# Squares of t as one ScalarE operation with their sum on VectorE, two of three bias-and-relu operations on ScalarE, and a new order of calls on four engines

## What is computed

```python
x = x + conv(_ln_c(x))            # norm over channels
#   per 3x3 patch: similarity of 9 pixels to 512 prototypes, argmax,
#   mix of best pixel and best prototype, an MLP (tanh, relu), a 1x1 conv, fold
t = _to_tokens(x)
def _ln_t(v, eps=1e-5):
    m = jnp.mean(v, axis=-1, keepdims=True)
    s = jnp.var(v, axis=-1, keepdims=True)
    return (v - m) / jnp.sqrt(s + eps)
q_mul = lambda x: _float_quantize(x, 5, 2)      # fp8 values
q_acc = lambda x: _float_quantize(x, 5, 10)     # fp16 values
def _qlinear(x, W, b):
    y = q_acc(jnp.einsum('bsk,nk->bsn', q_mul(x), q_mul(W)))
    return q_acc(y + q_mul(b))
h = jax.nn.relu(_qlinear(t_normed, W1, b1))     # 96 -> 384
y = _qlinear(h, W2, b2)                         # 384 -> 96
t = t + y
```

## Time and profile before

| | |
|---|---|
| median of 3 runs | 2089.93 us (2086.12 to 2092.7) |
| the profiled execution: its time | 2092.94 us |
| its span, first to last instruction | 2090.8 us |
| TensorE's mean granted clock | 0.981 of full |
| busy: TensorE | 1957.4 us, 94% |
| busy: VectorE | 2003.2 us, 96% |
| busy: ScalarE | 1829.2 us, 87% |
| busy: GpSimd | 1549.9 us, 74% |

### The profile page before, as it was taken

How to read it: one execution, slowest core, us unless ns; L and a number is a source line. 1 busy time by engine, 2 the same in 40 slices (tenths; PEclk the granted TensorE clock), 3 DMA queues, 4 the chain that set the end, 5 groups by cost and what they waited for, 6 DMA issues and landing times.

```text
span 2090.8 us, 46997 instructions
## 1 busy us (share of the span) xinstructions
PE 1957.4 (94%) x13105; PEld 1434.5 (69%) x13105; DVE 2003.2 (96%) x6781; ACT 1829.2 (87%) x5381; POOL 1549.9 (74%) x1042
## 2 busy tenths in 40 slices
PE   5899999999999999999999999999999999999975
PEld 4677777777777777767777777777777777777653
DVE  7999999999999999999999999999999999999953
ACT  1179999999999999999999999999999999999997
POOL 2577877878778777787887777878778778787753
PEclk9999999999999999999999999999999999999985
DMA  3322232332322323323233232232332322323111
GB/s 89 97 78 88 94 106 87 98 102 87 108 91 95 105 87 102 97 91 110 86 97 103 87 107 92 95 105 87 102 97 93 108 86 98 103 87 111 46 40 51
DMA packets 65475, 193.27 MB, mean 92 GB/s; under 512 B 13689, under 2 KB 15939, under 8 KB 65219
## 3 DMA queue, kind: packets, MB, share of 16 engines
q1 hardware_dynamic: 52866, 170.80, 25.2%
q0 software_dynamic: 10240, 18.89, 3.0%
q10 hardware_dynamic: 2112, 0.60, 0.1%
HBM read 133.23 MB, written 57.02 MB: 91 GB/s over the span
## 4 chain that ended last, share of the span: by engine, by line
DVE 89%; issue 6%; PE 3%; ACT 1%; POOL 0%; DMA 0%; POOLq 0%; ACTq 0%; DVEq 0%
DVE best_y L1026 28%; DVE h L1043 13%; DVE stats L1035 9%; DVE t_pm L1051 6%; DVE simraw L1077 6%; DVE top_v L1065 4%; DVE w_index L1072 4%; DVE zb L992 3%; DVE xn L984 1%; DVE mix_in L971 1%; DVE m_dif L929 1%; DVE r_u L1010 1%; DVE ra L1018 1%; DVE one_j L903 1%; DVE r_t L1015 1%
## 5 line engine op out<-in xcount | busy, mean ns | idle before, releaser
L1026 DVE TENSOR_REDUCE best_y<-y_ps 128x2 f32<-128x1024 f32 (+1 forms) x640 | 692.7, 1103 | 4.0 <-PE y_ps L651 3.9
L466 ACT CAST y<-bank 128x384 f16<-128x384 f32 x1152 | 550.5, 478 | 140.8 <-PE bank L674 129.8
L649 PE MATMUL y_ps<-proto_hi,xh 96*128 96x512 f32 x1152 | 553.8, 481 | 22.2 <-DVE best_y L1026 10.4
L359 POOL TENSOR_TENSOR tq<-t_dev,ra 128x864 fp8e5<-128x864 f32 x128 | 209.5, 1637 | 401.3 <-DVE ra L1018 401.3
L650 PE MATMUL y_ps<-proto_lo,xh 96*128 96x512 f32 x1152 | 458.4, 398 | 0.0
L651 PE MATMUL y_ps<-proto_hi,xl 96*128 96x512 f32 x1152 | 457.3, 397 | 0.0
L475 ACT ACTIVATE h<-h 128x1152 fp8e5<-128x1152 f16 x384 | 448.3, 1168 | 0.0
L674 PE MATMUL bank<-tqt,f_w 96*128 96x384 f16 x1152 | 390.4, 339 | 26.5 <-ACT y L466 24.6
L403 POOL TENSOR_TENSOR xl<-xc,xh 96x1152 fp32r<-96x1152 f32 x128 | 339.7, 2654 | 26.4 <-ACT xh L536 15.2
L1043 DVE TENSOR_SCALAR h<-y,f_b 128x1152 f16<-128x1152 f16 x384 | 306.1, 797 | 21.0 <-ACT y L466 20.9
L505 ACT ACTIVATE sq_junk<-t_dev 128x96 f32<-128x96 f32 x1152 | 318.8, 289 | 0.9 <-POOL t_dev L371 0.9
(11 more groups left out here) (131 smaller groups left out, 3997.3 us busy)
## 6 DMA issues: line engine op xcount, KB each, us to landing
xc<-x_cm SPq DMA_DIRECT2D x128, 432.0 KB, 4.0
xp<-x_pm SPq DMA_DIRECT2D x128, 432.0 KB, 4.8
out<-o_pm SPq DMA_DIRECT2D x128, 432.0 KB, 2.5
xsel<-x_pm,x_index POOLq DMA_INDIRECT x128, 2.5
wsel<-proto_rows,w_index POOLq DMA_INDIRECT x128, 4.9
proto_rows<-proto SPq DMA_DIRECT2D x1, 384.0 KB, 2.6
proto<-w_mask SPq DMA_DIRECT2D x1, 192.0 KB, 3.4
f_f<-w_1t ACTq DMA_DIRECT2D x1, 144.0 KB
```

The costliest lines, as they stand in the source:

```text
L466: act.copy(y16[:, q, r, 0:TOK], bank[0][:, 0:TOK]).then_inc(s_y16, 1)
L649: pe.matmul(y, hi, proto_hi[:], start=True, stop=False)
L1026: dve.tensor_reduce(best_y[t % 2][:, j0:j1], y_ps[n % 2][:, 0:j1 - j0, :], AX_X, ALU.max).then_inc(s_yd, 1)
```

## The change

The nine squares with an accumulator become one ACTIVATE over 864 columns, which writes t_sq; a new call t_squares on VectorE sums it by a TENSOR_REDUCE into va and raises s_sqd, for which variances and the next square wait. A new call hidden16 on ScalarE does the bias and relu by one ACTIVATE for q = 0 and q = 1 in stage FFN; VectorE keeps q = 2 in stage FFN2. The semaphore for h16 becomes three, one per q. The slot lists of GpSimd, ScalarE, TensorE and VectorE are put in another order.

```diff
@@ -115,7 +115,7 @@
 
         x_sums = [sb(f"x_sums{b}", [P, J, 2]) for b in range(RING)]
         mean_t = [sb(f"mean_t{b}", [P, J]) for b in range(2)]
-        sq_junk = sb("sq_junk", [P, JC])
+        t_sq = sb("t_sq", [P, JC])
 
 
         va = [sb(f"va{b}", [P, 4 * J]) for b in range(2)]
@@ -204,7 +204,8 @@
         s_cv = sem("conv_filled")
         s_t = sem("t_ready")
         s_mean = sem("mean_t_ready")
-        s_sq = sem("sq_t_ready")
+        s_sq = sem("t_sq_ready")
+        s_sqd = sem("t_sq_summed")
         s_rest = sem("rest_ready")
         s_wt = sem("wterm_ready")
         s_rt = sem("root_ready")
@@ -214,7 +215,7 @@
         s_tt = sem("tqt_ready")
         s_f1 = sem("ffn1_filled")
         s_y16 = sem("y16_ready")
-        s_h16 = sem("h16_ready")
+        s_h16 = [sem(f"h16_ready{q}") for q in range(NH)]
         s_h8 = sem("h8_ready")
         s_f2 = sem("ffn2_filled")
         s_z = sem("z16_ready")
@@ -424,14 +425,14 @@
                         in_offset=bass.IndirectOffsetOnAxis(ap=w_index[t % 2][:, 0:1], axis=0)).then_inc(s_wg[t % 2], 16)
 
             def slot(s):
+                gather_x(s)
                 lock(s)
                 t_norm(s)
                 product(s)
+                low_x(s)
                 t_center(s)
-                gather_x(s)
+                low_h(s)
                 output(s)
-                low_x(s)
-                low_h(s)
                 gather_w(s)
 
             run.slots(slot)
@@ -462,14 +463,25 @@
                     t = s - FFN
                     q, r = k // 3, k % 3
                     run.wait(s_f1, NC * t + k + 1)
-                    run.wait(s_h16, NH * (t - 1) + q + 1)
+                    run.wait(s_h16[q], t)
                     act.copy(y16[:, q, r, 0:TOK], bank[0][:, 0:TOK]).then_inc(s_y16, 1)
 
-            def hidden8(s, stage, q):
+            def hidden16(s, stage, q):
 
                 if run.live(s, stage):
                     t = s - stage
-                    run.wait(s_h16, NH * t + q + 1)
+                    run.wait(s_y16, NC * t + 3 * (q + 1))
+                    run.wait(s_h8, NH * (t - 1) + q + 1)
+                    run.apart()
+                    act.activation(h16[:, q, :, 0:P].rearrange("p (r j) l -> p r j l", r=3),
+                                   y16[:, q, :, 0:TOK].rearrange("p r (j l) -> p r j l", l=P), ACT.Relu,
+                                   bias=f1_b[:, q:q + 1]).then_inc(s_h16[q], 1)
+
+            def hidden8(s, stage, q):
+
+                if run.live(s, stage):
+                    t = s - stage
+                    run.wait(s_h16[q], t + 1)
                     run.wait(s_f2, 2 * (t - 1))
                     run.apart()
                     act.activation(h8[t % 2][:, q, :].rearrange("p (j l) -> p j l", l=P), h16[:, q, :, 0:P], ACT.Copy,
@@ -493,19 +505,14 @@
                     run.wait(s_f1, NC * (t - 1))
                     act.copy(tqt[t % 2][:, j0 * P:j1 * P], bank16[3 - n][0:C, 0:(j1 - j0) * P]).then_inc(s_tt, 1)
 
-            def squares(s, js):
+            def squares(s):
 
                 if run.live(s, CONV):
                     t = s - CONV
-                    for j in js:
-                        if j == 0:
-                            run.wait(s_dev, t + 1)
-                            run.wait(s_rt, s - MATCH)
-                            run.apart()
-                        ins = act.activation(sq_junk[:, j * C:(j + 1) * C], t_dev[t % 2][:, j * C:(j + 1) * C],
-                                             ACT.Square, accum_out=va[(s + 1) % 2][:, J + j:J + j + 1])
-                    if js[-1] == J - 1:
-                        ins.then_inc(s_sq, 1)
+                    run.wait(s_dev, t + 1)
+                    run.wait(s_sqd, t)
+                    run.apart()
+                    act.activation(t_sq[:], t_dev[t % 2][:], ACT.Square).then_inc(s_sq, 1)
 
             def vcs_out(s):
                 if run.live(s, HIDDEN):
@@ -563,33 +570,32 @@
                     act.activation(hid[:], bank[1][0:C, 0:NH * P], ACT.Relu).then_inc(s_hid, 1)
 
             def slot(s):
+                high(s)
                 ffn1_out(s, 0)
+                hidden8(s, FFN2, 1)
                 vcs_out(s)
                 ffn1_out(s, 1)
-                hidden8(s, FFN2, 1)
-                high(s)
+                hidden8(s, FFN2, 2)
                 ffn1_out(s, 2)
-                hidden8(s, FFN2, 2)
                 xnt_out(s)
+                hidden16(s, FFN, 0)
                 ffn1_out(s, 3)
+                hidden8(s, FFN, 0)
+                ffn1_out(s, 4)
                 layer1_out(s)
+                turned(s, 0)
+                ffn1_out(s, 5)
+                weighted(s)
                 mix_out(s)
-                weighted(s)
-                turned(s, 0)
-                ffn1_out(s, 4)
                 turned(s, 1)
+                ffn1_out(s, 6)
+                hidden16(s, FFN, 1)
                 hidden1_out(s)
-                ffn1_out(s, 5)
-                hidden8(s, FFN, 0)
-                squares(s, range(0, 2))
-                ffn1_out(s, 6)
-                squares(s, range(2, 4))
+                ffn1_out(s, 7)
+                squares(s)
                 ffn2_out(s, 0)
-                ffn1_out(s, 7)
+                ffn1_out(s, 8)
                 ffn2_out(s, 1)
-                squares(s, range(4, 7))
-                ffn1_out(s, 8)
-                squares(s, range(7, 9))
 
             run.slots(slot)
 
@@ -757,36 +763,36 @@
                     last.then_inc(s_i1, 1)
 
             def slot(s):
+                match(s, 0)
+                match(s, 1)
+                ffn1(s, 0)
                 hidden2(s)
-                ffn1(s, 0)
-                match(s, 0)
+                match(s, 2)
                 ffn1(s, 1)
+                match(s, 3)
+                turn_x(s)
...
@@ -952,7 +958,7 @@
                     if run.live(s, MATCH):
                         steps.need("norm")
                     if run.live(s, NORM):
-                        run.wait(s_sq, s - NORM + 1)
+                        run.wait(s_sqd, s - NORM + 1)
                         run.apart()
                     steps.done("va", dve.scalar_tensor_tensor(va[s % 2][:, 2 * J:], va[s % 2][:, 0:2 * J], 1.0 / C, eps[:],
                                                               ALU.mult, ALU.add))
@@ -1036,12 +1042,18 @@
                     if js[-1] == J - 1:
                         steps.done("x", ins)
 
+            def t_squares(s):
+                if run.live(s, NORM):
+                    run.wait(s_sq, s - NORM + 1)
+                    ins = dve.tensor_reduce(va[s % 2][:, J:2 * J], t_sq[:].rearrange("p (j c) -> p j c", c=C), AX_X, ALU.add)
+                    ins.then_inc(s_sqd, 1)
+
             def ffn_bias(s, stage, q):
                 if run.live(s, stage):
                     t = s - stage
                     run.wait(s_y16, NC * t + 3 * (q + 1))
                     dve.tensor_scalar(h16[:, q, :, 0:P], y16[:, q, :, 0:TOK], f1_b[:, q:q + 1], 0.0, ALU.add,
-                                      ALU.max).then_inc(s_h16, 1)
+                                      ALU.max).then_inc(s_h16[q], 1)
 
             def residual(s, n):
                 if run.live(s, CONV):
@@ -1078,21 +1090,21 @@
                         simraw[:], prod[:].rearrange("p (j c) -> p j c", c=C), AX_X, ALU.add))
 
             def slot(s):
-                low_part(s)
+                t_squares(s)
                 x_dif(s)
+                x_sum(s)
+                x_sq(s)
+                cos(s)
                 mix_sims(s)
-                cos(s)
-                x_sq(s)
-                ffn2_bias(s)
-                x_sum(s)
                 x_norm(s)
-                mix_row(s)
                 best_j(s)
                 ffn_bias(s, FFN2, 2)
                 variances(s)
+                one_hot(s)
+                low_part(s)
+                mix_row(s)
+                root(s, 0)
                 normed_x(s)
-                root(s, 0)
-                one_hot(s)
                 root(s, 1)
                 pick_mean(s)
                 root(s, 2)
@@ -1100,25 +1112,24 @@
                 root(s, 3)
                 root(s, 4)
                 root(s, 5)
+                ffn2_bias(s)
                 pick_root(s)
                 root(s, 6)
+                y_max(s, 0)
                 residual(s, 0)
                 residual(s, 1)
+                remainder(s)
                 t_mean(s)
-                y_max(s, 0)
-                remainder(s)
                 y_max(s, 1)
-                ffn_bias(s, FFN, 0)
                 x_stats(s, [0, 1, 2])
                 x_stats(s, [3, 4])
+                y_max(s, 2)
                 sims(s)
+                y_max(s, 3)
+                best_v(s)
                 x_stats(s, [5])
-                y_max(s, 2)
-                best_v(s)
+                v_index(s)
                 x_stats(s, [6, 7, 8])
-                ffn_bias(s, FFN, 1)
```

(40 more changed lines are left out.)

## The result

The changed kernel takes **2067.98 us** (median of 4 runs, 2064.44 to 2069.78); the kernel before, run beside it, 2088.26 (2086.12 to 2092.7). The ratio is 0.9889 with a 95% interval of 0.9868 to 0.9911: faster by 1.1%, where 3% was forecast. The direction was right; the time lies above the range of 2012 to 2062. The profiled execution took 2069.78 us, 23.2 under the one of before, where the sum had -62.

The account below looks back on a forecast made before the run. VectorE's instruction list was taken as the bound, its slot falling from 15.38 to 14.81 us: 118 x 0.57 = -67, +2 for thin margins, +3 tail, 2092.9 to 2031 us, 2028 as median; range 2012 to 2062.

Parts of the forecast that it names:

- the sum: Whole run: -67 us over 118 slots, +2 for thin margins, +3 in the tail, from the profiled 2092.9 to 2031 us.
- The bound: Mid-run slot: VectorE's list stays the bound, 15.38 to 14.81 us, and VectorE waits for nobody, margins 0.3 to 0.6 us.
- B: Rival: the engines lock step at 15.1 to 15.2 us a slot, -37 us, about 2055 us; chance 0.16.
- C: Rival: ScalarE becomes the bound and keeps its 1.0 us waits for ffn1's product, slot 15.7, 2123 us; chance 0.08.
- D: Rival: ScalarE reaches the square one long operation (1.25 us) late, slot 15.42, 2089 us, no change; chance 0.04.
- The removed and added operations: VectorE's list: two bias-and-relu operations go, 1.44 us; one TENSOR_REDUCE comes in, 0.95; net -0.49 us a slot.
- ScalarE's list: ScalarE per slot: squares and accumulator reads -2.43, one square +0.81, two relus +2.30; +0.68 us, to 14.6 to 14.9.
- Moved: VectorE's reordered list: x_norm saves 0.11 us, x_sq costs 0.03; elsewhere operations needing a result have another ahead, as before.
- It costs nothing: GpSimd's gather_x ahead of the lock: free, as the index is out about 1.1 us before root, as long as the gather takes.
- the ring through the squares: Root, GpSimd's t_norm to t_center, ScalarE's square, VectorE's sum, root again: closes in 14.1 us, 0.7 under VectorE's slot.
- The tail: Drain, bounded by ScalarE: +4 us from +0.68 in about six slots, -1 for the relu; +3 us, bounds -4 and +10.

Follow-up runs that it names:

- experiment 2: Changed kernel with GpSimd's gather of xsel moved from ahead of the lock back behind t_center: 2106.55 us, ratio 1.0063.
- experiment 1: Changed kernel with only VectorE's calls reordered, to put more or longer operations between short ones and their producers: 2040.94 us, ratio 0.9755.
- experiment 6: Both changes of operations, with the calls of all four engines in the order of the kernel before: 2373.51 us (one run).
- experiment 8: Changed kernel with the nine squares and accumulators back on ScalarE in a row, without t_squares; relus and order as changed: 2197.09 us (one run).
- experiment 4: Changed kernel with the sum of squares over only 8 of the 96 channels, to shorten VectorE's list alone: 2024.09 us (one run).
- experiment 9: Changed kernel with VectorE's calls spaced and the gather of xsel behind t_center: 2088.36 us (one run), the kernel before 2093.54 beside it.
- experiment 3: Changed kernel with all three relus on VectorE in the drain only (slots 130 and later): 2071.9 us, ratio 0.9895.
- experiment 5: Kernel with spaced VectorE calls, with ffn2_bias (zb) moved behind root: 2044.59 us, ratio 0.9764 against the kernel before the change.
- experiment 7: Changed kernel with all three bias-and-relu operations on VectorE again, squares and new order kept: 2310.49 us (one run).

## Why the prediction was wrong, and where it was right

**The bound** held. The forecast said that VectorE's list stays the bound, with nobody waited for; its busy share is 99.8% (which by itself proves little: in experiment 2, where x_dif is held, it is 99.5%), and moving nothing but VectorE's calls (experiment 1) shortened the slot by 0.20. Rivals B, C and D did not come about; the waits that B and C lived on are gone. The relu alone is dearer on ScalarE, 1.26 against 0.80 us, as C had it; the change gains all the same, since ScalarE had the room and VectorE had none. Experiment 6 shows how much hangs on the order: with the same operations in the old one the kernel is 13% slower than before the change. (B's 118 x 0.3 is 35 us, not 37; its time moves by 2 us, and nothing hangs on it.)

**The removed and added operations** were sized right: the relu on VectorE 0.71 to 0.72, the sum 0.96 instead of 0.95, the relu on ScalarE 1.26, the square 0.93, and the pairs at 0.27 (experiment 8). ScalarE's list was put at 14.6 to 14.9 us and comes to 14.50 by the estimate of experiment 8.

**The step that failed** is "Moved": -0.11 for x_norm, +0.03 for x_sq, and the sentence that elsewhere "every operation that needs a result has another ahead of it, as before". In the new list the operations in between are too few or too short: around x_sum, x_sq, x_norm and v_index the distances are 0.12 to 0.22, together with pick_root 0.24 us a slot over the forecast. That is 27 of the 39 us. Of the 0.24, results that are needed make 0.15; the 0.05 at cos went too when the calls were spaced, though it needs none of them, and the 0.03 at pick_root stayed. With the short steps spaced, the slot was 14.84 us against the forecast's 14.81, and the time, 2040.94, lies inside the range that the changed kernel missed. That it is so close is in part luck, since pick_root and the longer x_dif, 0.03 and 0.05 us, were not in the forecast.

**"It costs nothing"** of the gather ahead of the lock was wrong as well, though it is not in the miss: the index is out 1.1 us before the root, but the gather starts 0.84 us after it and takes 0.94. That is 0.43 us in the ring through the squares, which had 0.7 of room. And it was the right place all the same: behind t_center the gather delays o_pm by 1 us, and o_pm blocks x_dif. This second ring was not in the forecast at all. It stays 0.36 us under the list in the changed kernel; it is what bounds experiments 2, 4 and 9.

**The two held gathers** cost 5.7 us, a cost that is absent where the gather stands behind t_center. It does not show in the balance, since the small hiccups of before went: over the 108 slots, what exceeds the median slot is 7.6 us after and 6.5 before. In every kernel with the gather ahead of the lock (the changed one and experiments 1, 3, 4, 5, 7 and 8) it is the same two gathers, the 58th and the 113th of 128, and each starts 2.67 or 2.68 us later behind its index than the others, at whatever time of the run it comes. Where the gather stands behind t_center these two are not late. So the place in the program sets it and not the moment; what holds them there is open.

**The tail** was put at +3 and came out at +11. The term rested on ScalarE, and experiment 3 took the relus away from it and got a longer tail; experiment 6, with the old order and the new operations, has 133.6 us. So putting back neither the relus nor the order alone brings the 115.6 back; the recorded test of experiment 6 points at the relus, experiment 3 against them. The granted clock of the first 100 us of the drain goes along with it only in part: 0.74 before, 0.71 after, 0.73 in experiment 1 (tails of 115.6, 126.8 and 122.7 us), 0.63 in experiment 3 (135.3), 0.66 in experiments 2 and 5 (128.6 and 128.7), 0.82 in experiment 9 (121.2), but 0.75 in experiment 7, whose tail is 126.6. Among kernels with the changed order a lower clock mostly goes with a longer tail, yet even at 0.82 the tail is over the 115.6 that the kernel before took at 0.74. TensorE is busy for as long in it:

```profile
1941.00:2041.00 100.00, 73.75 (x462) 52.69 (x460) 42.40 (x135) 91.16 (x162) 45.48 (x32) 0.71 0.10 40
```
```profile
1975.00:2075.00 100.00, 72.49 (x463) 49.05 (x461) 49.01 (x145) 89.86 (x262) 47.22 (x33) 0.74 0.11 42
```

(The first is the changed kernel, the second the one before.) The cause of the 8 us stays open. So do the 5 us at the start. The granted clock averaged 0.97 up to tile 10 before and 0.93 after (0.70 between 50 and 75 us, where the kernel before had 0.91), but experiment 6 took 173.6 us there at 0.97. Other kernels that share the changed order lie at 169 to 180 us, and no single edit was made for it.

## What to carry to other kernels

Count a saturated engine's list in distances from start to start, and ask of each short operation how much work lies between it and its producer: one short one was not enough here, 0.2 to 0.3 us were, and that alone was worth 1.3% (2067.98 to 2040.94). When four engines are within a few per cent of one another, the order of calls decides more than the operations: the same ones gave +13%, -1.1% and -2.4%. Before moving a call on GpSimd, look at which two-input VectorE operations the tensor operations behind it will then meet; a blocked one shows as a long duration, never as a wait.

## What the runs showed of the hardware that was not expected

- x_dif, a VectorE operation with both inputs in SBUF, ends 0.04 us after the GpSimd tensor operation in which it starts, however short it is itself: 0.58, 0.63 and 0.71 us for nine columns that take 0.17. The profile counts this as VectorE's busy time. Where it starts only 0.05 us before the end of o_pm (experiment 5), it keeps its 0.17. The sum, with one input, and the residual, with one of two in a bank, keep their length.
- A gather issued by GpSimd starts 0.84 us after the semaphore that it waits for, a tensor operation 0.20, and it lasts 0.94 to 0.99. Beside a long two-input operation on VectorE (zb, experiment 5) it lasts 1.12, and pick_root on VectorE lasts 216 ns instead of 162 where it starts together with the gather.
- Short VectorE operations that nothing holds follow one another after 0.08 us. One that needs a result starts no earlier than some 0.03 after its producer's end (x_sq here; x_norm in the earlier trace rows), and a load of match values no earlier than 0.15 after it (both loads). Why cos, which needs neither x_dif nor x_sq, comes 0.13 behind x_sq in the changed kernel and no longer when the list is spaced, was not tried.
